# The scaling of the second norm's token rows on ScalarE: eight copies with a factor per partition

## The chip, the cores and the metric

The kernel runs on one core of one Trainium2 chip. The metric is the device time of one execution in microseconds. The kernel before took 679.23, 679.91 and 679.58 us in three runs, a median of 679.58.

## What is computed

One block of a vision tower over 4 images of 64 channels and 64 x 64 pixels, in float32. `h` starts as an involution (a 3 x 3 filter whose weights are computed from the pixel), with a class token ahead of it; a state-space layer on its norm is added; and last an expert layer on its second norm is added. The change lies in this last part:

```
h = h + ffn(layernorm(h))
ffn: H = gelu(x @ W1 + b1)                      64 -> 256 channels
     probs = softmax(H @ Wg + bg)               8 experts
     e = argmax(probs)
     out = probs[e] * (H @ Wd[e] + bd[e])       256 -> 64 channels
```

The layer norm has no weights: (x - mean) / sqrt(var + 1e-5) over the 64 channels of a token. The kernel takes the mean into W1 (a centering matrix is multiplied into it), so the rows only have to be multiplied by the factor 1 / sqrt(var + 1e-5).

## The kernel before

Stages with a barrier between them: set-up, involution, matrices of the state-space layer, its norm, the layer itself, and `experts` (line 1204). The change touches `experts` alone.

**Items.** The 16384 tokens are cut into 16 items of 1024 tokens, and a 17th has the four class tokens. `hT` holds the channels on partitions, with two tokens (a "par" each) side by side on 128 partitions, 512 columns an item. An item passes these steps; the letters in brackets name the engine.

- `turn_in` (L1316) [TensorE]: four transposes bring tokens onto partitions; `rest` (L1490) [ScalarE] copies the result out of PSUM into `hs`: 128 partitions x 8 groups x 64 channels.
- `minus_sum` (L1539) [VectorE] and `squares` (L1469) [ScalarE, eight activations with an accumulated sum] give sum and variance of every token; `factor` (L1675 to L1685) [GpSimd, six instructions on 128 x 8] gives the factor, `fac`.
- `normalise` (L1552) [VectorE]: one product of the 128 x 512 rows of `hs` with `fac`, broadcast along the channels, gives `xn`.
- `turn_out` (L1324) [TensorE]: four transposes back; `high` (L1461) [ScalarE] and `low` (L1545) [VectorE] split the result into a high part and a remainder, `u`.
- `hide(i, h)` for h = 0, 1 (L1335) [TensorE]: six matmuls with W1 into the two banks `pH`; `gelu(i, h)` (L1446) [ScalarE] reads each bank twice, four activations of 512 columns; `part` (L1531) [VectorE] makes the remainder.
- `judge` (L1351) [TensorE], `add_bg` (L1477) and `tanh` (L1483) [ScalarE], `gates` (L1361) [TensorE], `choose_best` and `weigh_best` (L1563 to L1595) [VectorE]: the gate.
- `speak(i, t)` for eight tiles t (L1382) [TensorE]: six matmuls give all eight experts' outputs of 128 tokens into one of three banks `pE`; `multiply(i, t)` (L1525) [VectorE] multiplies them by the gate, which is zero for all experts but one.
- `tree(i, k)` for k = 0, 1 (L1694, L1696, L1698, L1703) [GpSimd]: sums over the eight experts for four tiles, and adds `hs`; `keep_bias` (L1601) and `finish` (L1610) [VectorE] add the bias; a DMA stores the rows.

**The order.** Each engine's program is written out by hand as a loop over windows i = -3 to 16, and the engines meet only at semaphores; an engine carries out its own instructions in their order. In window i:

- TensorE: hide(i+1, 0), speak 0 and 1 of item i, hide(i+1, 1), speak 2, the transposed gate, turn_out(i+2), speak 3 and 4, judge(i+1), speak 5, gates(i+1), speak 6, the bias matmul, turn_in(i+4), speak 7. `hide(i, h)` waits until the gelus before it have emptied the banks (L1331); `speak` waits until the multiply three tiles earlier has emptied its bank (L1377); `judge` waits for all four `part` of the item (L1342).
- ScalarE: gelu(i+1, 0), gelu(i+1, 1), the copy of the gate, high(i+2), squares(i+3), add_bg(i+1), tanh(i+1), rest(i+4); in the very first window then two casts of the bias table (L1511, L1512).
- VectorE: multiply 0, keep_bias(i-1), part, multiply 1, part, minus_sum(i+3), multiply 2, two part, multiply 3, finish(i-1), multiply 4, low(i+2), multiply 5, choose_best(i+1), multiply 6, weigh_best(i+1), multiply 7, and last normalise(i+3). Behind the first window stands a subtraction on the bias table (L1662), which waits for the casts.
- GpSimd: tree(i, 0), factor(i+3), tree(i, 1). The first tree waits for multiply 3 (L1692), the factor for squares(i+3).

`normalise(i)` waits for `factored` of its item and for `turned_out` of the item before, since there is one `xn`; `turn_out(i)` waits for `normed`.

Of the kernel before, what the change touches and what calls it, by code (L numbers as in the profile page):

```python
# [6 lines left out]
ALU = mybir.AluOpType  # L7
ACT = mybir.ActivationFunctionType
# [7 lines left out]
F = HW  # L16
# [1187 lines left out]
def experts(nc, g):  # L1204
# [3 lines left out]
    NH = 6  # L1208
# [4 lines left out]
    with ExitStack() as ctx:  # L1213
        def sem(name):
            return ctx.enter_context(nc.semaphore("ex_" + name))

        def sb(name, shape, dt=F32):
            return ctx.enter_context(nc.sbuf_tensor("ex_" + name, shape, dt))
# [17 lines left out]
        hs = [sb(f"hs{n}", [128, TPI, F]) for n in range(NH)]  # L1236
# [3 lines left out]
        fac = [sb(f"fac{n}", [128, 4, TPI]) for n in range(2)]  # L1240
        xn = sb("xn", [128, TPI, F])
# [24 lines left out]
        newton, factored, normed = sem("newton"), sem("factored"), sem("normed")  # L1266
        turned_out, u_high, u_made = sem("turned_out"), sem("u_high"), sem("u_made")
# [14 lines left out]
        def there(i):  # L1282
            return 0 <= i < ITEMS

        def is_cls(i):
            return i == NCH

        def cols(i):
            return B if is_cls(i) else CH

        def rows(i):
            return B if is_cls(i) else 128

        def columns(i):
            return 1 if is_cls(i) else TILES

        def groups(i):
            return 2 * columns(i)

        def tiles(i):  # L1300
            return 1 if is_cls(i) else TPI
# [4 lines left out]
        with nc.Block() as block:  # L1306
# [129 lines left out]
            @block.scalar  # L1436
            def _(act):
                def gelu(i, h):
                    if i >= 2:
                        act.wait_ge(spoke, TPI * (i - 1))  # L1440
                    if i >= 1:
                        act.wait_ge(parted, 4 * (i - 1) + 2 * h + 2)
                    for par in range(2):
                        act.wait_ge(hidden, 4 * i + 2 * h + par + 1)
                        for o in (hidf, hid[i % 2][0]):
                            last = nc.scalar.activation(o[:, h, par, 0:cols(i)], pH[par][:, 0:cols(i)], ACT.Gelu,  # L1446
                                                        bias=g.b1c[:, h:h + 1])
                        last.then_inc(gelued, 1)

                def keep_gate(i):  # L1450
                    act.wait_ge(gate_turned, i + 1)
                    if i >= 1:
                        act.wait_ge(biased, i)
                    P = rows(i)
                    nc.scalar.copy(gT[:, 0:P], pT[:, 0:P]).then_inc(gate_kept, 1)

                def high(i):
                    act.wait_ge(turned_out, i + 1)
                    if i >= 2:
                        act.wait_ge(hidden, 4 * (i - 1))  # L1460
                    nc.scalar.copy(u[i % 2][0][:, 0:cols(i)], pXU[:, 0:cols(i)]).then_inc(u_high, 1)  # L1461

                def squares(i):
                    act.wait_ge(summed, i + 1)
                    if i >= 2:
                        act.wait_ge(factored, i - 1)
                    P = rows(i)
                    for t in range(groups(i)):
                        last = nc.scalar.activation(sq[0:P, i % 2, t, :], hs[i % NH][0:P, t, :], ACT.Square, scale=float(F),  # L1469
                                                    bias=stat[i % 2][0:P, 0, t:t + 1], accum_out=stat[i % 2][0:P, 1, t:t + 1])  # L1470
                    last.then_inc(squared, 1)

                def add_bg(i):
                    act.wait_ge(judged, i + 1)
                    if i >= 1:
                        act.wait_ge(gated, i)
                    nc.scalar.activation(level[:, 0:cols(i)], pGR[0:4 * EX, 0:cols(i)], ACT.Identity,  # L1477
                                         bias=g.bgc[:, 0:1]).then_inc(leveled, 1)

                def tanh(i):  # L1480
                    act.wait_ge(dv, GATE * i + 3)
                    P, T = rows(i), groups(i)
                    nc.scalar.activation(gl[0:P, 2, 0:T], gl[0:P, 0, 0:T], ACT.Tanh, scale=0.5).then_inc(tanhed, 1)  # L1483

                def rest(i):
                    act.wait_ge(turned_in, i + 1)
                    if i >= NH:
                        act.wait_ge(reduced, NB * (i - NH + 1))
                    P, n = rows(i), 128 * columns(i)
                    nc.scalar.copy(hs[i % NH][0:P, 0:groups(i), :].rearrange("p t f -> p (t f)"), pXU[0:P, 0:n]).then_inc(rested, 1)  # L1490

                act.wait_ge(w1_made, 1)
                nc.scalar.copy(W1P[0][:], pH[0][:, 0:HID]).then_inc(w1_made, 1)
                rest(0)
                for i in range(1 - AHEAD, ITEMS):
                    if there(i + 1):
                        gelu(i + 1, 0)
                        gelu(i + 1, 1)
                    if there(i):
                        keep_gate(i)  # L1500
                    if there(i + 2):
                        high(i + 2)
                    if there(i + 3):
                        squares(i + 3)
                    if there(i + 1):
                        add_bg(i + 1)
                        tanh(i + 1)
                    if there(i + 4):
                        rest(i + 4)
                    if i == 1 - AHEAD:  # L1510
                        nc.scalar.copy(bdh[lower], bd[lower])  # L1511
                        nc.scalar.copy(bdP[upper], bd[upper]).then_inc(bd_high, 1)  # L1512

            @block.vector
            def _(v):
# [26 lines left out]
                def low(i):  # L1542
                    v.wait_ge(u_high, i + 1)
                    c = slice(0, cols(i))
                    nc.vector.tensor_tensor(u[i % 2][1][:, c], pXU[:, c], u[i % 2][0][:, c], ALU.subtract).then_inc(u_made, 1)  # L1545

                def normalise(i):
                    P, T = rows(i), groups(i)
                    v.wait_ge(factored, i + 1)
                    if i >= 1:  # L1550
                        v.wait_ge(turned_out, i)
                    nc.vector.tensor_tensor(xn[0:P, 0:T, :], hs[i % NH][0:P, 0:T, :], fac[i % 2][0:P, 3, 0:T].unsqueeze(2).broadcast_to([P, T, F]),  # L1552
                                            ALU.mult).then_inc(normed, 1)

                def choose_best(i):
                    P, T = rows(i), groups(i)
# [56 lines left out]
                def window(i):  # L1613
                    now = tiles(i) if there(i) else 0
                    more = there(i + 1)
                    if now:
                        multiply(i, 0)
                    if there(i - 1):
                        keep_bias(i - 1)
                    if more:  # L1620
                        part(i + 1, 0, 0)
                    if now > 1:
                        multiply(i, 1)
                    if more:
                        part(i + 1, 0, 1)
                    if there(i + 3):
                        minus_sum(i + 3)
                    if now > 2:
                        multiply(i, 2)
                    if more:  # L1630
                        part(i + 1, 1, 0)
                        part(i + 1, 1, 1)
                    if now > 3:
                        multiply(i, 3)
                    if there(i - 1):
                        finish(i - 1)
                    if now > 4:
                        multiply(i, 4)
                    if there(i + 2):
                        low(i + 2)  # L1640
                    if now > 5:
                        multiply(i, 5)
                    if more:
                        choose_best(i + 1)
                    if now > 6:
                        multiply(i, 6)
                    if more:
                        weigh_best(i + 1)
                    if now > 7:
                        multiply(i, 7)  # L1650
                    if there(i + 3):
                        normalise(i + 3)

                nc.vector.memset(inverse[:, :, EX:], -float(EX)).then_inc(consts, 1)
                v.wait_ge(consts, 1)
# [109 lines left out]
```

## Time and profile before

| | us |
|---|---|
| median of three runs | 679.58 |
| lowest and highest | 679.23, 679.91 |
| the profiled execution, time | 679.56 |
| its span | 677.8 |
| TensorE busy | 593.3 (88%) |
| VectorE busy | 531.1 (78%) |
| GpSimd busy | 410.4 (61%) |
| ScalarE busy | 266.4 (39%) |

The span runs from the first to the last instruction that the profiler recorded; the device time is 1.8 us longer. The expert stage begins at 363 us of the span. Busy shares are means over all stages.

How to read the rows further down: PE is TensorE's matmuls, PEld its weight loads, DVE VectorE, ACT ScalarE, POOL GpSimd; L1552 is line 1552 of the kernel; after the arrow in brackets stands whose work ended the idle time before the instruction. On ScalarE, VectorE and TensorE an instruction's duration includes some tail that overlaps the next one's start, so the distance of two starts tells what an instruction costs in a row of its like.

### The profile page before, as it was taken

The numbers are of one execution on the slowest core, as the hardware profiler recorded it, in microseconds if no ns is written. First come the engines' busy times: TensorE is split into PE (matmuls) and PEld (weight loads), VectorE is DVE, ScalarE is ACT, GpSimd is POOL, SyncE is SP. The second block draws the span as 40 slices with busy tenths as digits, with TensorE's granted clock in tenths as the row PEclk, the third lists the DMA queues.
The fourth block names the chain that finished last, engine by engine and source line by source line (L and its number), as shares of the span: only waits on it lengthen the run. The fifth ranks groups of instructions, "written<-read, shape, count | busy, mean of one in ns | idle before, by whom it ended". The sixth has DMA issues, their size and how long they took to land. (4 is left out here: it accounts for less than half of the span.)

```text
span 677.8 us, 9715 instructions
## 1 busy us (share of the span) xinstructions
PE 593.3 (88%) x2998; PEld 436.9 (64%) x2998; DVE 531.1 (78%) x966; ACT 266.4 (39%) x691; POOL 410.4 (61%) x562
## 2 busy tenths in 40 slices
PE   0699999966995799999984599999999999999994
PEld 0477777754763688778763277766666666766672
DVE  6688888873596688888871378898889988888985
ACT  2132223223473122222223765555555555555310
POOL 1689999610154043333336248888878778888777
PEclk9999999995795999999997599999999999999998
DMA  6200000000000000000000000000000000000001
GB/s 252 49 2 0 0 1 1 0 0 1 0 0 1 0 1 0 1 0 0 1 0 0 1 1 16 16 17 15 17 15 12 6 15 16 17 16 16 15 17 31
DMA packets 13140, 9.78 MB, mean 14 GB/s; under 512 B 4524, under 2 KB 12844, under 8 KB 12844
## 3 DMA queue, kind: packets, MB, share of 16 engines
q1 hardware_dynamic: 13084, 9.29, 4.3%
q8 instruction: 19, 0.31, 0.2%
q14 instruction: 21, 0.17, 0.1%
q10 hardware_dynamic: 16, 0.00, 0.0%
HBM read 5.10 MB, written 4.20 MB: 14 GB/s over the span
## 5 line engine op out<-in xcount | busy, mean ns | idle before, releaser
L1382 PE MATMUL ex_pE<-ex_WdP,ex_hid 128*128 128x512 f32 x774 | 203.7, 405 | 0.0
L1382 PEld LDWEIGHTS ex_pE<-ex_WdP,ex_hid 128*128 128x128 f32 x774 | 138.8, 187 | 41.7 <-issue 10.9
L1694 POOL TENSOR_TENSOR ex_s<-ex_ms 128x1024 f32<-128x1024 f32 (+1 forms) x33 | 84.3, 2554 | 46.8 <-DVE ex_ms L1525 46.8
L1525 DVE TENSOR_TENSOR ex_ms<-ex_pE,ex_gate 128x512 f32<-128x512 f32 x129 | 87.8, 682 | 22.9 <-PE ex_pE L1382 22.5
L1195 POOL TENSOR_TENSOR hT<-hT,ssm_gelu 128x512 f32<-128x512 f32 x32 | 47.7, 1508 | 94.8 <-ACT ssm_gelu L1168 94.8
L723 DVE TENSOR_TENSOR inv_prod<-inv_pW,m_img 128x504 f32<-128x504 f32 x144 | 91.7, 681 | 17.1 <-PE inv_pW L638 15.4
L649 PE MATMUL inv_pS<-ident,inv_prod 128*128 128x128 f32 x576 | 87.5, 274 | 4.7 <-DVE inv_prod L723 4.7
L649 PEld LDWEIGHTS inv_pS<-ident,inv_prod 128*128 128x128 f32 x576 | 69.8, 140 | 27.2 <-DVE inv_prod L723 19.3
L638 PE MATMUL inv_pW<-inv_ysb,m_conv2L 98*128 98x512 f32 x144 | 69.4, 485 | 2.3 <-DVE inv_ysb L711 2.3
L1446 ACT ACTIVATE ex_hidf<-ex_pH,b1c 128x512 f32<-128x512 f32 (+1 forms) x68 | 45.1, 663 | 55.9 <-PE ex_pH L1335 55.9
L1151 ACT CAST ssm_z<-ssm_back 128x512 fp32r<-128x512 f32 x32 | 18.3, 618 | 101.5 <-DVE ssm_back L1127 101.5
L1065 PE MATMUL ssm_y<-ssm_z,N 128*128 128x512 f32 x192 | 51.9, 407 | 6.7 <-DVE ssm_z L1130 6.5
L1130 DVE TENSOR_TENSOR ssm_z<-ssm_back,ssm_z 128x512 fp32r<-128x512 f32 x32 | 36.1, 1170 | 19.3 <-ACT ssm_z L1151 19.3
L1531 DVE TENSOR_TENSOR ex_hid<-ex_hidf,ex_hid 128x512 fp32r<-128x512 f32 (+1 forms) x68 | 50.2, 758 | 1.2 <-ACT ex_hid L1446 1.2
L1032 PE MATMUL ssm_v<-u,LV 128*128 128x512 f32 (+1 forms) x192 | 50.5, 409 | 0.0
L1696 POOL TENSOR_TENSOR ex_s<-ex_s 128x512 f32<-128x512 f32 (+1 forms) x33 | 46.7, 1416 | 2.6
L1065 PEld LDWEIGHTS ssm_y<-ssm_z,N 128*128 128x128 f32 x192 | 36.5, 193 | 17.6 <-DVE ssm_z L1130 9.2
L1469 ACT ACTIVATE ex_sq<-ex_hs,ex_stat 128x64 f32<-128x64 f32 (+1 forms) x130 | 43.5, 345 | 7.1 <-DVE ex_stat L1539 7.1
L800 POOL TENSOR_TENSOR u<-ln_u,u 128x512 fp32r<-128x512 f32 x14 | 18.6, 1350 | 44.6 <-ACT u L869 44.6
L1446 ACT ACTIVATE ex_hid<-ex_pH,b1c 128x512 fp32r<-128x512 f32 (+1 forms) x68 | 45.2, 665 | 0.0
L1552 DVE TENSOR_TENSOR ex_xn<-ex_hs,ex_fac 128x512 f32<-128x512 f32 (+1 forms) x17 | 33.1, 1946 | 14.8 <-POOL ex_fac L1685 14.8
L1351 PE MATMUL ex_pGR<-ex_hid,ex_WgP 128*32 128x512 f32 (+1 forms) x136 | 34.4, 396 | 9.1 <-DVE ex_hid L1531 9.0
(242 smaller groups left out, 1048.3 us busy)
## 6 DMA issues: line engine op xcount, KB each, us to landing
m_img<-in_x SPq DMA_DIRECT2D x2, 2048.0 KB, 9.2
out<-ex_res SPq DMA_DIRECT2D x16, 256.0 KB, 2.2
WdT<-in_L_ffn_Wd SPq DMA_DIRECT2D x2, 256.0 KB
bd<-in_L_ffn_bd SPq DMA_DIRECT2D x16, 2.0 KB
W1d<-in_L_ffn_W SPq DMA_DIRECT2D x2, 64.0 KB
m_Bm<-in_L_attn_fwd_B_real SPq DMA_DIRECT2D x2, 16.0 KB, 2.0
m_Bm<-in_L_attn_fwd_B_imag SPq DMA_DIRECT2D x2, 16.0 KB, 2.0
m_Bm<-in_L_attn_bwd_B_real SPq DMA_DIRECT2D x2, 16.0 KB, 2.0
```

Source lines behind the costliest of these rows:

```text
L638: nc.tensor.matmul(pW[k % NW][:], m.conv2L[:, k, :], ysb[u][:], start=True, stop=True).then_inc(weighed, 1)
L649: last = nc.tensor.matmul(pS[:, 128 * j:128 * j + 128], prod[:, k, 2 * j:2 * j + 2, :], g.ident[:], is_transpose=True, start=(k == 0 and j ...
L723: nc.vector.tensor_tensor(prod[:, k, :, lo:hi], pW[k % NW][:, :, lo:hi], rows[:, :, lo + dw:hi + dw], ALU.mult).then_inc(filtered, 1)
L1032: last = nc.tensor.matmul(out[:], g.LV[weight][:, LVI[d][t][q], :], cols(g.u[value], b, d, h, q), start=(q == 0 and (value, weight) == PAR ...
L1065: last = nc.tensor.matmul(out, g.N[weight][:, n, d, first:first + 2, :], before(zP[n][value], d, h), start=False, stop=(n == 1 and (value, ...
L1195: nc.gpsimd.tensor_tensor(t, t, act_y[n % 4][:], ALU.add).then_inc(summed, 1)
L1382: last = nc.tensor.matmul(pE[n % 3][0:P].rearrange("p e f -> p (e f)"), hid[i % 2][value][:, h, par, 128 * j:128 * j + P], WdP[weight][:, ...
L1446: last = nc.scalar.activation(o[:, h, par, 0:cols(i)], pH[par][:, 0:cols(i)], ACT.Gelu, bias=g.b1c[:, h:h + 1])
L1525: nc.vector.tensor_tensor(ms[b % NB][0:P, t % TPB, :].rearrange("p (e f) -> p e f", e=EX), pE[n % 3][0:P], gate[i % 2][0:P, t, :].unsqueez ...
L1531: nc.vector.tensor_tensor(hid[i % 2][1][:, h, par, c], hidf[:, h, par, c], hid[i % 2][0][:, h, par, c], ALU.subtract).then_inc(parted, 1)
L1694: nc.gpsimd.tensor_tensor(s4[0:P, 0:T], m[:, :, 0:4 * F], m[:, :, 4 * F:], ALU.add).then_inc(halved, 1)
L1696: nc.gpsimd.tensor_tensor(s2[0:P, 0:T], s4[0:P, 0:T, 0:2 * F], s4[0:P, 0:T, 2 * F:], ALU.add).then_inc(quartered, 1)
```

## The change

The one VectorE product in `normalise` is replaced by up to eight ScalarE activations of the function Copy, one for each of the groups of 64 channels, each with its column of `fac` as a scale that is read per partition. The waits are the same. On VectorE the step stood at the end of window i, behind multiply 7; on ScalarE it stands at the end of window i too, behind `rest(i+4)`, and in the first window ahead of the two casts.

```diff
@@ scalar engine
+                def normalise(i):
+                    act.wait_ge(factored, i + 1)
+                    if i >= 1:
+                        act.wait_ge(turned_out, i)
+                    P = rows(i)
+                    for t in range(groups(i)):
+                        last = nc.scalar.activation(xn[0:P, t, :], hs[i % NH][0:P, t, :], ACT.Copy, scale=fac[i % 2][0:P, 3, t:t + 1])
+                    last.then_inc(normed, 1)
...
                     if there(i + 4):
                         rest(i + 4)
+                    if there(i + 3):
+                        normalise(i + 3)
                     if i == 1 - AHEAD:
                         nc.scalar.copy(bdh[lower], bd[lower])
@@ vector engine
-                def normalise(i):
-                    P, T = rows(i), groups(i)
-                    v.wait_ge(factored, i + 1)
-                    if i >= 1:
-                        v.wait_ge(turned_out, i)
-                    nc.vector.tensor_tensor(xn[0:P, 0:T, :], hs[i % NH][0:P, 0:T, :], fac[i % 2][0:P, 3, 0:T].unsqueeze(2).broadcast_to([P, T, F]),
-                                            ALU.mult).then_inc(normed, 1)
...
                     if now > 7:
                         multiply(i, 7)
-                    if there(i + 3):
-                        normalise(i + 3)
```

## Rows read from the trace of the kernel before

**Rows 1.** The page: busy us, share of the span and instructions.

```profile
PE 593.3 (88%) x2998; PEld 436.9 (64%) x2998; DVE 531.1 (78%) x966; ACT 266.4 (39%) x691; POOL 410.4 (61%) x562
```

**Rows 2.** The chain of waits: start us, us, engine, tile, line.

```profile
594.84 2.80 POOL ex_s L1694
...
612.73 2.80 POOL ex_s L1694
```

**Rows 3.** Timeline, same turn: start us, us, engine, line, operation [idle before].

```profile
594.84 2.79 POOL L1694 TENSOR_TENSOR ex_s<-ex_ms 128x1024 f32<-128x1024 f32 x1 [2.48 <-DVE ex_ms L1525]
...
603.55 0.20 POOL L1685 TENSOR_TENSOR ex_fac<-ex_fac 128x8 f32<-128x8 f32 x1
...
603.78 2.87 DVE L1552 TENSOR_TENSOR ex_xn<-ex_hs,ex_fac 128x512 f32<-128x512 f32 x1 [0.36 <-POOL ex_fac L1685]
...
606.58 0.68 DVE L1525 TENSOR_TENSOR ex_ms<-ex_pE,ex_gate 128x512 f32<-128x512 f32 x1
...
611.97 0.68 DVE L1525 TENSOR_TENSOR ex_ms<-ex_pE,ex_gate 128x512 f32<-128x512 f32 x1
```

**Rows 4.** Timeline of TensorE's weight loads: `hide(.., 1)` of windows 1, 2, 13, 14.

```profile
411.05 0.53 PEld L1335 LDWEIGHTS ex_pH<-ex_u,ex_W1P 64*128 64x128 f32 x6 [0.37 <-issue]
...
428.07 0.53 PEld L1335 LDWEIGHTS ex_pH<-ex_u,ex_W1P 64*128 64x128 f32 x6 [0.37 <-issue]
...
623.07 0.53 PEld L1335 LDWEIGHTS ex_pH<-ex_u,ex_W1P 64*128 64x128 f32 x6 [0.37 <-issue]
...
640.45 0.53 PEld L1335 LDWEIGHTS ex_pH<-ex_u,ex_W1P 64*128 64x128 f32 x6 [0.37 <-issue]
```

**Rows 5.** Timeline of ScalarE, two gelus of the class tokens, 4 columns.

```profile
657.23 0.26 ACT L1446 ACTIVATE ex_hid<-ex_pH,b1c 128x4 fp32r<-128x4 f32 x1
657.38 0.26 ACT L1446 ACTIVATE ex_hidf<-ex_pH,b1c 128x4 f32<-128x4 f32 x1
```

**Rows 6.** Timeline, first and fourth gelu of item 0, the weight load behind them.

```profile
377.38 0.69 ACT L1446 ACTIVATE ex_hidf<-ex_pH,b1c 128x512 f32<-128x512 f32 x1 [0.44 <-PE ex_pH L1335]
...
379.10 0.70 ACT L1446 ACTIVATE ex_hid<-ex_pH,b1c 128x512 fp32r<-128x512 f32 x1
...
379.91 0.95 PEld L1335 LDWEIGHTS ex_pH<-ex_u,ex_W1P 64*128 64x128 f32 x6 [3.29 <-issue]
```

**Rows 7.** Groups of ScalarE by form, scale and bias by pointer: busy, mean ns.

```profile
L673 ACT ACTIVATE inv_yf<-inv_pY,m_ysc 96x512 f32<-96x512 f32 x16 | 12.4, 775 | 17.7 <-PE inv_pY L629 17.7
```

**Rows 8.** Timeline of window 0: `hide(1, 1)`, first tree, last factor instruction.

```profile
394.03 0.54 PEld L1335 LDWEIGHTS ex_pH<-ex_u,ex_W1P 64*128 64x128 f32 x6 [0.37 <-issue]
...
399.37 2.40 POOL L1694 TENSOR_TENSOR ex_s<-ex_ms 128x1024 f32<-128x1024 f32 x1 [9.12 <-DVE ex_ms L1525]
...
407.70 0.20 POOL L1685 TENSOR_TENSOR ex_fac<-ex_fac 128x8 f32<-128x8 f32 x1
```

**Rows 9.** Timeline of the fill, windows -3 to 0: casts, normalise, squares, gelu.

```profile
369.22 0.62 ACT L1512 CAST ex_bdP<-bd 64x512 fp32r<-64x512 f32 x1
...
371.32 0.69 DVE L1552 TENSOR_TENSOR ex_xn<-ex_hs,ex_fac 128x512 f32<-128x512 f32 x1 [6.01 <-POOL ex_fac L1685]
372.04 0.69 DVE L1662 TENSOR_TENSOR ex_bdP<-bd,ex_bdh 64x512 fp32r<-64x512 f32 x1
...
373.70 0.35 ACT L1469 ACTIVATE ex_sq<-ex_hs,ex_stat 128x64 f32<-128x64 f32 x1
...
379.63 0.69 DVE L1552 TENSOR_TENSOR ex_xn<-ex_hs,ex_fac 128x512 f32<-128x512 f32 x1 [5.10 <-POOL ex_fac L1685]
...
391.20 0.69 ACT L1446 ACTIVATE ex_hidf<-ex_pH,b1c 128x512 f32<-128x512 f32 x1
```

**Rows 10.** Timeline of TensorE in the state-space stage, a long wait.

```profile
355.22 2.93 PE L1065 MATMUL ssm_y<-ssm_z,N 128*128 128x512 f32 x6 [2.86 <-DVE ssm_z L1130]
```

**Rows 11.** Busy time by stretch; after the brackets the granted clock's share.

```profile
355.00:356.50 1.50, 1.28 (x3) 1.10 (x4) 0.16 (x1) 0.00 (x0) 1.30 (x1) 0.50 0.00 0
```

**Rows 12.** Groups of ScalarE by form, a load of an activation table.

```profile
L357 ACT ACT_TABLE_LOAD x1 | 1.3, 1283 | 3.3 <-issue 3.3
```

## The prediction

> **What bounds the kernel now.** I read the page's busy table first. TensorE is busy for 88% of the span and ScalarE for 39% [rows 1]; that invites the thought that work moved to ScalarE is free. A share of the whole span cannot say that, so I read the chain of waits next. In the expert stage it repeats every 17.89 us: first half-tile tree of GpSimd, its factor computation, a stretch called "issue", VectorE's work, the same tree again [rows 2]. The kernel there is no queue of one engine but a loop through GpSimd and VectorE.
>
> The timeline of one turn gives its parts [rows 3]. I write T for the start of the first tree of a window. T is 594.84; the factors are ready at 603.75, 8.91 later; `normalise` starts on VectorE at 603.78 and holds it until the next multiply at 606.58, 2.80; from that multiply to the fourth one are 5.39; this one takes 0.68 and the next tree starts 0.08 after it. 8.91 + 0.03 + 2.80 + 5.39 + 0.76 = 17.89. So `normalise` is on the path, with all of its 2.80 us.
>
> The weight loads of the second half of `hide` tell how long the windows are [rows 4]. I call their start H. While TensorE itself is the limit, H comes every 17.02 us (411.05 to 428.07). From H = 411.05 (window 1) to H = 623.07 (window 13) are 212.02 us for twelve windows, 17.67 each: only 0.65 each, 7.8 in all, above what TensorE needs. That is all that a free normalise could give back there.
>
> **The removed part.** VectorE loses 2.80 us per window in the loop above, and everything behind it in its queue (multiply, bias, part) moves forward. The old loop shrinks to 15.1 and no longer binds.
>
> **The added part: eight copies.** The trace before has no ScalarE copy of 64 columns with a pointer to its factor. The nearest rows are the gelus, which have one pointer too (the bias). With 4 columns they follow each other at 0.15 us [rows 5], with 512 columns at (379.10 - 377.38) / 3 = 0.573 [rows 6], so a column costs 0.8 ns and 64 of them cost 0.15 + 0.05 = 0.20. Lower end: 0.15, if the 60 columns more are free. Upper end: an activation with two pointers lasts 775 ns [rows 7] against the 0.69 of a gelu, 0.09 more; if the copy has a second pointer too it is 0.29. I take 0.20, the form being the gelu's: 8 x 0.20 = 1.60 before the next instruction of ScalarE starts, with bounds 1.2 and 2.3; xn itself is complete at 7 x 0.20 + 0.31 = 1.71. The Trainium skill's page "ScalarE: Activation LUTs" (What ACT_TABLE_LOAD costs) gives 186 ns + 0.833 per column, 93 for a pointer and an overlap of 93; an estimate by it is 0.24 a copy, 1.92 for eight, and would put the sum below about 5 us higher. The same page (Rules for kernel authors) says to use VectorE for a plain multiplication; no row here shows the copy, and the sum below tests that rule in its place in the loop.
>
> **The added wait, and what stands behind it.** ScalarE's queue is in order. At the end of window i it now waits for the factors of item i+3, and behind that wait stand the four gelus of `gelu(i+2, 0)`. `hide(i+2, 1)` waits for these gelus, and behind it on TensorE stand all matmuls of the next `speak`. So a second loop comes into being:
>
> T to factors ready 8.91 [rows 3], hand-over 0.04, copies 1.60, four gelus 379.80 - 377.38 = 2.42, last gelu to weight load 379.91 - 379.80 = 0.11 [rows 6], H to the next T 399.37 - 394.03 = 5.34 [rows 8]. Sum 18.42.
>
> The last term is of window 0, where little but TensorE's order lies in it (hide, third speak, turn-out, fourth speak, then VectorE's fourth multiply). VectorE's other work of that stretch (bias, the first parts, the negative sum) fits before its third multiply, since VectorE comes 2.8 us earlier; GpSimd's second tree falls there too and may block a `part` for some tenths, which I leave to the range.
>
> 18.42 is above 17.02 and above 17.67. Twelve windows: H(13) - H(1) = 221.0 where it was 212.0, +9.0.
>
> **Window 0.** T to factors is 407.90 - 399.37 = 8.53 [rows 8], so H(1) = H(0) + 5.34 + 8.53 + 0.04 + 1.60 + 2.42 + 0.11 = H(0) + 18.04, where it was 17.02: +1.0.
>
> **The start.** Here the copies hurt most, because the pipeline is being filled and ScalarE's order is all there is. (a) `normalise(0)` runs at 371.32 [rows 9], for only 0.69 here, where GpSimd is quiet, and now until 372.93 on ScalarE, and the two casts of the bias table (0.62 each) come behind it: done at 374.17, not at 369.84. VectorE's subtraction that waits for them (0.69, begun at 372.04 before) ends at 374.9, the negative sum behind it at 375.6, and the squares of item 1 start at 375.65, not at 373.70: 1.95 late. (b) The factors of item 1 were ready just before `normalise(1)` at 379.63 [rows 9]; now at 381.58. ScalarE waits for them, copies until 383.2, and only then begins `gelu(0, 0)`, which had begun at 377.38 [rows 6], 2.2 before those factors existed: 5.8 late. From there `hide(0, 1)`, judge, gates and the rest of item 3 follow 5.8 late. (c) `normalise(2)` stands ahead of `gelu(1, 0)`: 391.20 [rows 9] + 5.8 + 1.6 = 398.6; gelus and hand-over 2.53, so H(0) = 401.13, where it was 394.03 [rows 8]: +7.1. Bounds: +5.5 if (a) is hidden, +9 with the upper price of a copy.
>
> **The end.** Item 16 has 4 rows and two copies of 0.2, so window 13 is TensorE's again: at most 17.02, where 640.45 - 623.07 = 17.38 [rows 4]: -0.4. Behind it nothing changes.
>
> No DMA is moved; the stores wait for `finish` and move with the windows. The pointer buffers (`fac`, `hs`, `xn`) have at least as long to live as before; `turned_out(i)` is given in the middle of the window and is no wait.
>
> **Sum.** +7.1 + 1.0 + 9.0 - 0.4 = +16.7, over 679.56, the profiled execution's time (span 677.8; the three runs' median is 679.58, the same): 696.3, and I say 696.5. The price of a copy counts eight-fold in 15 places: 1.2 instead of 1.60 gives 690, 2.3 gives 707. Contention of `part` with the second tree could add up to 0.3 in 12 windows, 4.
>
> **Rivals.**
>
> 1. *The relief wins.* ScalarE is idle for 61% [rows 1], the copies vanish in it, and the windows fall to 17.02: 679.6 - 7.8 - 0.4 = 671.4. This decides if the new loop stays within 17.02: 18.42 less the 1.60 of the copies is 16.82, so all eight copies would have to take 0.2 us together, or the factors to be ready 1.4 us earlier. The idle share of ScalarE speaks for it, the loop against it. 3 in 100.
>
> 2. *The loops balance.* The new loop equals the old windows of 17.67 if the eight copies take 0.85 together, 0.11 each; with a start that hides its waits the time would be some 680. The price of a gelu with 4 columns, 0.15 [rows 5], speaks against it. 3 in 100.
>
> 3. *Copies as dear as with two pointers*, or a longer one from SBUF: 2.3 per window, 705 to 708. 10 in 100.
>
> 4. *TensorE's clock falls.* The copies make it stand still for some 1.4 us more before H. The trace has one wait of 2.86 us, and behind it six matmuls took 2.93 us [rows 10] at a granted clock of 0.50, the lower level [rows 11]. If each window brought that, about 2 us more in 13 windows: 722. The new wait is half as long. 3 in 100.
>
> 5. *A table load for the copy*, 1.28 us as other functions had in the set-up [rows 12], once before the copies and once behind them in each window, 15 times: 39 more, 735. In the expert stage square, gelu, tanh and identity follow each other, and the trace has no load there. 1 in 100.
>
> **How the numbers follow.** The forecast has 80 in 100 and its time is 696.5. The range goes from the lower price of a copy, 690, to the upper one, 707, and leaves rivals 1, 2, 4 and 5 out. About 0.2% (1.4 us) can be told from no change. Faster 0.03, the same 0.03, slower 0.94.
>
> **What would show it.** In the profile after: (i) windows 1 to 13 about 18.4 us apart, H(1) near 419, H(13) near 640; (ii) the chain goes from the factors to ScalarE's copies and gelus, then TensorE's `hide` and `speak`, with no VectorE stretch of 2.8; (iii) `hide(.., 1)` waits for gelus, about 1.4 us; (iv) the wait of `judge` for `part` is gone; (v) the gelus of item 0 start near 383. Windows of 17.0 would make the loop wrong; windows of 18.4 with a start unchanged would make the steps (a) to (c) wrong; another pitch of copies only the price.

## The result and the profile after

The changed kernel takes 708.98 us in the median of four executions (703.59 to 713.02), the kernel before 679.75 in the four beside them. The ratio, which is not the quotient of the two medians, is 1.0405 (95% interval 1.0308 to 1.0503): slower. The direction was forecast; the size was not. The forecast was 696.5 with a range to 707; the profiled execution, at 703.59, lies inside it, the median 2 us above. Of the executions of the kernel before that stand beside the experiments, one took 1462.28 us; what held it up is not known, and ratios leave it out.

The page of the kernel after, its busy line (against [rows 1]). ScalarE gains only 3 points, and no engine is busier than 84%:

```profile
PE 592.8 (84%) x2998; PEld 438.8 (63%) x2998; DVE 510.6 (73%) x949; ACT 297.1 (42%) x821; POOL 406.1 (58%) x562
```

The chain of waits of the kernel after, one turn (start us, us, engine, tile, line; the lines behind 1498 are shifted by 1 on GpSimd and by 11 or less on VectorE, so L1695 is the first tree, L1678 the factor's power, L1536 the multiply):

```profile
511.75 1.78 ACT ex_xn L1498 x7
515.26 0.58 ACT ex_hid L1446
515.98 0.97 PE ex_pH L1335 x6
516.94 1.59 PE ex_pE L1382 x6
519.08 1.42 PE ex_pE L1382 x6
520.53 0.70 DVE ex_ms L1536
521.30 2.79 POOL ex_s L1695
...
527.45 1.66 POOL ex_fac L1678
530.51 1.78 ACT ex_xn L1498 x7
```

It is the loop of the forecast: first tree, factors, copies, gelus, `hide`, two `speak`, the fourth multiply, the tree. It repeats after 18.76 us where the old one took 17.89 [rows 2]. VectorE has one instruction in it.

The timeline of the same turn gives the terms (against [rows 3]):

```profile
511.26 0.20 POOL L1686 TENSOR_TENSOR ex_fac<-ex_fac 128x8 f32<-128x8 f32 x1
511.50 2.04 ACT L1498 ACTIVATE ex_xn<-ex_hs,ex_fac 128x64 f32<-128x64 f32 x8 [1.85 <-POOL ex_fac L1686]
...
513.44 0.67 ACT L1446 ACTIVATE ex_hidf<-ex_pH,b1c 128x512 f32<-128x512 f32 x1
...
515.15 0.68 ACT L1446 ACTIVATE ex_hid<-ex_pH,b1c 128x512 fp32r<-128x512 f32 x1
...
515.95 0.56 PEld L1335 LDWEIGHTS ex_pH<-ex_u,ex_W1P 64*128 64x128 f32 x6 [2.08 <-issue]
515.98 0.97 PE L1335 MATMUL ex_pH<-ex_u,ex_W1P 64*128 64x512 f32 x6 [1.67 <-ACT ex_hid L1446]
...
521.30 2.78 POOL L1695 TENSOR_TENSOR ex_s<-ex_ms 128x1024 f32<-128x1024 f32 x1 [3.21 <-DVE ex_ms L1536]
...
530.02 0.20 POOL L1686 TENSOR_TENSOR ex_fac<-ex_fac 128x8 f32<-128x8 f32 x1
```

Tree to factors 530.22 - 521.30 = 8.92; hand-over 0.04; copies 513.44 - 511.50 = 1.94; four gelus 515.83 - 513.44 = 2.39; to the weight load 0.12; from there to the tree 5.35. The sum is 18.76. All terms but the copies are within 0.03 of the forecast's; the copies take 1.94, not 1.60. TensorE waits 1.67 us for the last gelu, where about 1.4 was expected. The wait of `judge` for `part`, 23.3 us in all before, is down to 4.7.

Where the 24.0 us between the two profiled spans went, by the starts of `hide(.., 1)` (H) and the first instruction of the expert stage. From here on, window i of a profile is the stretch from H(i) to H(i+1):

| stretch | before | after | difference | forecast |
|---|---|---|---|---|
| start of the span to the expert stage | 362.86 | 364.41 | +1.5 | 0 |
| to H(0) | 31.17 | 39.32 | +8.2 | +7.1 |
| H(0) to H(1) | 17.02 | 18.35 | +1.3 | +1.0 |
| H(1) to H(13) | 212.02 | 225.14 | +13.1 | +9.0 |
| H(13) to H(14) | 17.38 | 16.60 | -0.8 | -0.4 |
| to the end | 37.35 | 37.98 | +0.6 | 0 |

H(1) stands at 422.08 and H(13) at 647.22, where 419 and 640 were forecast; the windows are 18.76 and not 18.4.

### The profile page after: what moved, and what is told of

Same layout as the page of the kernel before. It is cut to its first block and busy times, and to the rows that moved or that the text cites. A ratio compares the mean times of both kernels' runs of the same rounds, so it can differ in the third digit from the quotient of the medians.

```text
span 701.8 us, 9828 instructions
## 1 busy us (share of the span) xinstructions
PE 592.8 (84%) x2998; PEld 438.8 (63%) x2998; DVE 510.6 (73%) x949; ACT 297.1 (42%) x821; POOL 406.1 (58%) x562
## 5 line engine op out<-in xcount | busy, mean ns | idle before, releaser
L1536 DVE TENSOR_TENSOR ex_ms<-ex_pE,ex_gate 128x512 f32<-128x512 f32 x129 | 88.4, 687 | 55.2 <-PE ex_pE L1382 52.9
L1695 POOL TENSOR_TENSOR ex_s<-ex_ms 128x1024 f32<-128x1024 f32 (+1 forms) x33 | 82.8, 2509 | 67.7 <-DVE ex_ms L1536 67.7
L1542 DVE TENSOR_TENSOR ex_hid<-ex_hidf,ex_hid 128x512 fp32r<-128x512 f32 (+1 forms) x68 | 57.8, 870 | 18.2 <-ACT ex_hid L1446 18.1
L1335 PE MATMUL ex_pH<-ex_u,ex_W1P 64*128 64x512 f32 (+1 forms) x204 | 33.2, 429 | 30.3 <-ACT ex_hid L1446 30.3
L1498 ACT ACTIVATE ex_xn<-ex_hs,ex_fac 128x64 f32<-128x64 f32 (+1 forms) x130 | 33.2, 338 | 31.8 <-POOL ex_fac L1686 31.8
L1335 PEld LDWEIGHTS ex_pH<-ex_u,ex_W1P 64*128 64x128 f32 x204 | 17.9, 192 | 44.5 <-issue 43.4
L688 ACT COPY hT<-inv_pS 128x256 f32 (+1 forms) x32 | 10.5, 383 | 81.9 <-PE inv_pS L649 81.9
```

The lines of the kernel that those rows point to most:

```text
L1335: last = nc.tensor.matmul(pH[par][:, 0:cols(i)], W1P[weight][r, 128 * h:128 * h + 128], u[i % 2][value][r, 0:cols(i)], start=((value, weig ...
L1498: last = nc.scalar.activation(xn[0:P, t, :], hs[i % NH][0:P, t, :], ACT.Copy, scale=fac[i % 2][0:P, 3, t:t + 1])
L1536: nc.vector.tensor_tensor(ms[b % NB][0:P, t % TPB, :].rearrange("p (e f) -> p e f", e=EX), pE[n % 3][0:P], gate[i % 2][0:P, t, :].unsqueez ...
L1542: nc.vector.tensor_tensor(hid[i % 2][1][:, h, par, c], hidf[:, h, par, c], hid[i % 2][0][:, h, par, c], ALU.subtract).then_inc(parted, 1)
L1695: nc.gpsimd.tensor_tensor(s4[0:P, 0:T], m[:, :, 0:4 * F], m[:, :, 4 * F:], ALU.add).then_inc(halved, 1)
```

## The experiments

Two things were open: whether the loss is the loop through the copies, and what makes executions of one kernel differ by 10 us. The times of the kernel before beside the first four runs are 675.90 to 684.72, median 680.73 (680.39 without the execution of 1462.28), and beside the others nearly the same; so 0.2% is finer than these runs tell.

**The changed kernel again.** No edit.

> The changed kernel unchanged, for its spread: four executions took 703.59 to 713.02, with a mean granted clock of 0.941 in the fastest and 0.920 in the slowest. Theory clock: the spread is TensorE's clock, which falls in some windows of some executions while TensorE waits before hide(.., 1); then the executions lie between 703.5 and about 714, their times rise with a falling mean clock (about 9 us for 0.02), and a profile of a slower one has stretches at 0.50 in the expert stage. Rival chance: the spread is of the machine and comes in other stages too; then the profile's extra time does not stand in the expert stage and the times do not follow the clock.

Six executions: 703.06 to 711.83, median 710.59, ratio 1.0430 (1.0376 to 1.0485); mean granted clocks 0.936 in the fastest, 0.922 in the slowest. The profile is of an execution of 707.81. Its windows 1 to 12 are 18.71 to 18.73 us but for two, 461.08 to 481.38 and 481.38 to 501.68, of 20.30. TensorE's timeline in the first of them, and the granted clock there (the third number from the right):

```profile
461.12 0.96 PE L1335 MATMUL ex_pH<-ex_u,ex_W1P 64*128 64x512 f32 x6 [1.65 <-ACT ex_hid L1446]
462.00 2.53 PE L1382 MATMUL ex_pE<-ex_WdP,ex_hid 128*128 128x512 f32 x6
...
464.54 1.06 PE L1324 MATMUL ex_pXU<-ident,ex_xn 128*128 128x128 f32 x4
```

```profile
461.00:462.00 1.00, 0.89 (x6) 0.53 (x6) 1.00 (x3) 0.00 (x0) 1.00 (x1) 1.00 0.00 0
...
464.00:465.00 1.00, 1.00 (x6) 0.80 (x5) 0.43 (x1) 0.81 (x3) 0.00 (x0) 0.50 0.00 0
...
466.00:467.00 1.00, 1.00 (x6) 0.81 (x5) 0.46 (x1) 1.00 (x6) 0.00 (x0) 1.00 0.00 0
```

Behind a wait of 1.65 us the six matmuls of `hide` still ran at 2.4 GHz; then the granted clock fell to 0.50, the level of 1.2 GHz, and the next six matmuls took 2.53 us. In the first profile of this kernel a wait of 1.77 us in the same window had no such effect:

```profile
459.71 0.96 PE L1335 MATMUL ex_pH<-ex_u,ex_W1P 64*128 64x512 f32 x6 [1.77 <-ACT ex_hid L1446]
460.61 1.67 PE L1382 MATMUL ex_pE<-ex_WdP,ex_hid 128*128 128x512 f32 x6
```

So the clock falls in some windows of some executions, at 1.57 us a time. It does not make up the whole difference: of the 4.2 us by which this execution is longer than the first profile, 3.1 are the two windows and 1.4 the start, where the clock rose later and H(0) stands 40.77 us behind the stage's start, not 39.32.

**The copies moved behind the first gelus.**

```diff
-                        gelu(i + 1, 1)
+                    if there(i + 2):
+                        normalise(i + 2)
+                    if there(i + 1):
+                        gelu(i + 1, 1)
...
-                    if there(i + 3):
-                        normalise(i + 3)
```

> The eight copies of item i+2 stand between gelu(i+1, 0) and gelu(i+1, 1) of window i, where ScalarE waits for hide(i+1, 1) anyway, not at the end of window i-1. Theory loop: the time of the changed kernel comes from the copies and the wait for the factors ahead of gelu(.., 0); moved behind it they leave the loop, windows fall to TensorE's 17.0 us, the start is about 1.5 us behind the kernel before: 671 to 675, faster than both, spread small. Rival price: a ScalarE activation of 64 columns is dear wherever it stands; then windows stay above 18 us and the time above 690.

Twelve executions: 669.07 to 678.03, median 675.85 beside 680.73, ratio 0.9916 (0.9883 to 0.9948). Windows 0 to 11 are 17.01 to 17.02 us long. The timeline shows why: the copies begin when the fourth gelu of the first half has been given out, and `hide(.., 1)` starts during them:

```profile
518.34 0.70 ACT L1446 ACTIVATE ex_hid<-ex_pH,b1c 128x512 fp32r<-128x512 f32 x1
518.91 2.02 ACT L1498 ACTIVATE ex_xn<-ex_hs,ex_fac 128x64 f32<-128x64 f32 x8
519.42 0.53 PEld L1335 LDWEIGHTS ex_pH<-ex_u,ex_W1P 64*128 64x128 f32 x6 [0.37 <-issue]
520.82 0.68 ACT L1446 ACTIVATE ex_hidf<-ex_pH,b1c 128x512 f32<-128x512 f32 x1
```

The same eight copies, as dear as before, cost nothing here: the place in ScalarE's queue is what costs. The median missed the expected 671 to 675 by 0.9 us, and the spread, 9.0 us, is not small. In the profiled execution the start was 3.9 us longer than before (H(0) 35.11 behind the stage's start, against 31.17), not 1.5. The gelus of item 0 begin 1.5 us late, as expected; the copies of item 1 ahead of `gelu(0, 1)` add 0.4; and about 2 come from the clock, which rose later in this execution: `turn_in`, `hide(1, 0)` (1.65 us, not 0.97) and the first two `speak` ran wholly or partly at 1.2 GHz.

**Every copy twice.**

```diff
+                        nc.scalar.activation(spare[0:P, t, :], hs[i % NH][0:P, t, :], ACT.Copy, scale=fac[i % 2][0:P, 3, t:t + 1])
                         last = nc.scalar.activation(xn[0:P, t, :], hs[i % NH][0:P, t, :], ACT.Copy, scale=fac[i % 2][0:P, 3, t:t + 1])
```

> Every copy is made twice, the second time into a tile that nobody reads; all else as in the changed kernel. Theory loop: each window grows by the whole 1.95 us, from 18.75 to 20.7, and the start by twice that: about +29 us, 733, in an execution whose clock stays up. Theory clock: the wait of TensorE before hide(.., 1) grows from 1.7 to 3.6 us, so the clock falls in many or all windows: 745 or more, and the granted clock of the expert stage well below 1. Rival slack: ScalarE has room and the loop is elsewhere; then under 715.

Median 757.29 (750.08 to 758.33), ratio 1.1141 (1.1083 to 1.1198), mean clock 0.90 to 0.91. One window of the profile, window 8 (582.58 to 603.20), is 20.62 us long, 1.87 above 18.75: nearly the whole 1.94 of the eight copies. The nine others of windows 3 to 12 are 22.08 to 22.23, 1.5 more, and there the clock fell to its lower level behind the longer wait (windows 1 and 2, at 23.23 and 23.53, are longer still):

```profile
516.12 1.65 PE L1336 MATMUL ex_pH<-ex_u,ex_W1P 64*128 64x512 f32 x6 [3.55 <-ACT ex_hid L1447]
517.70 1.65 PE L1383 MATMUL ex_pE<-ex_WdP,ex_hid 128*128 128x512 f32 x3
```

**The first three items on VectorE.** Items 0 to 2 keep the old product in its old place.

```diff
-                    if there(i + 3):
+                    if i >= 0 and there(i + 3):
                         normalise(i + 3)
...
+                    if i < 0:
+                        normalise(i + 3)
```

> Items 0 to 2 are normalised by VectorE as before the change, items 3 to 16 by ScalarE's copies. Theory loop with the fill priced by itself: the start is that of the kernel before, windows 1 to 13 stay at 18.75 us; 703.6 minus 7 to 8.5: 695 to 697 with the clock up. Rival: the fill's delay is hidden behind something later, then 702 to 704.

Median 700.14 (696.03 to 704.28), ratio 1.0291 (1.0225 to 1.0358). H(0) stands 31.16 us behind the start of the stage, as in the kernel before to 0.01, and windows 1 to 10 are 18.7 to 18.8. The fastest execution is 7.0 us below the fastest of the changed kernel. So 7 to 8 us of the change's cost are the start, by its three normalisations alone. Windows 11 and 12 of this profile are 20.28 and 20.32 and window 13 is 18.19 in place of 16.6: falls of the clock.

**TensorE kept busy in its wait.**

```diff
+                    if now == TPI and more:
+                        n = TPI * i + 2
+                        if n >= 3:
+                            pe.wait_ge(chosen, n - 2)
+                        for _ in range(10):
+                            nc.tensor.matmul(pE[n % 3][:].rearrange("p e f -> p (e f)")[:, 0:HID], W1P[0][:, 0:128], W1P[0][:],
+                                             start=True, stop=True)
                     if more:
                         hide(i + 1, 1)
```

> Ahead of hide(i+1, 1) TensorE makes ten matmuls of 256 columns more into the PSUM bank that speak 2 overwrites next, about 1.1 us that lie inside its wait of 1.67 us for the gelus; results unchanged. Theory clock: the executions of the changed kernel above 703 are those in which the clock falls in this wait, 1.57 us a time (windows of 20.30 instead of 18.73 in the profile of the run again); kept busy it does not fall, so the time is about 703 with a spread of 1 or 2 us above it, median 703 to 706 where the changed kernel had 710, mean clock at 0.93 or above. Rival chance: the spread and the median stay at 703 to 712. Rival issue: the added matmuls push hide(.., 1) back, then the windows of the profile are longer than 18.8.

Median 707.44 (701.37 to 709.45), ratio 1.0348 (1.0305 to 1.0390), mean clocks 0.930 to 0.946. Windows 1 to 12 are 18.73 to 18.75. In the stretches H(13) to H(14) and H(14) to H(15) (i = 14 and 15 of the edit), where no wait had been, the added matmuls cost 1.2 us each (17.78 and 17.19 for 16.59 and 16.00). The median is 1.4 above the expected 703 to 706; less these 2.4 it lies inside. The run was made again without them, with the changed kernel as its partner:

> The changed kernel once more, as the partner of the next run on the same chip. Theory clock: executions between 703 and 713, median about 710, mean clock 0.92 to 0.93 in the slower ones; a profile above 704 has windows of 20.3 us among those of 18.7.

> The ten added matmuls of 256 columns stand only in windows 0 to 13, where TensorE waits for the gelus, and no more in windows 14 and 15, where nothing waits and they cost 1.2 us each. Theory clock: as in the first run of this kind but 2.4 us less: median 704 to 706, fastest 699 to 701, 4 to 6 us below its partner; all windows of the profile 18.7. Rival chance: no difference to the partner beyond 1 us.

The changed kernel: median 707.16 (705.52 to 712.20), ratio 1.0375 (1.0321 to 1.0428), windows 2 and 3 of 20.33 and 20.32 and window 13 of 18.12 in place of 16.60. Kept busy: median 704.43 (699.55 to 706.42), ratio 1.0308 (1.0256 to 1.0361), no window of 1 to 13 above 18.75. The difference of the medians is 2.7 us, less than the 4 to 6 expected, and that of the means is 4.7 (708.35 and 703.63); the intervals of the ratios overlap. Ahead of H(0) the added matmuls met no wait in this profile and cost something there too: H(0) stands 41.95 us behind the stage's start, 40.22 in its partner. That the clock falls behind the wait is shown by the profiles. That filling the wait prevents it fits them (two of the three of the changed kernel have windows of 20.3, neither of the two with the filled wait has one), but so few profiles do not prove it, and what the falls cost in the median, some 3 to 5 us, is uncertain by as much.

Another part of the spread comes ahead of what the change touches: the expert stage began at 358.9 to 367.7 us in these profiles, and the kernel before has a spread of 9 us too. The slowest profile of the changed kernel, at 712.20, is 8.6 us above the first: 4.7 by its three falls, 3.3 by the later start of the stage, 0.9 by the time to H(0).

**The scale as a constant, and as a bias.**

```diff
-                        last = nc.scalar.activation(xn[0:P, t, :], hs[i % NH][0:P, t, :], ACT.Copy, scale=fac[i % 2][0:P, 3, t:t + 1])
+                        last = nc.scalar.activation(xn[0:P, t, :], hs[i % NH][0:P, t, :], ACT.Copy, scale=0.5)
```

> The eight copies multiply by a constant, 0.5, and not by the factor of the row; the wait for the factors stays. The computation is changed: the rows are not scaled by their factors. Theory pointer: a copy costs 0.24 us because of its pointer, 0.15 to 0.16 without it; then the windows are 0.6 to 0.7 us shorter, 18.1, and the fastest execution about 694. Rival source: the 0.24 is that of any small activation from SBUF; windows stay at 18.7 and the fastest at 703. Theory loop, in either case: windows shorten by eight times what one copy saves.

```diff
-                        last = nc.scalar.activation(xn[0:P, t, :], hs[i % NH][0:P, t, :], ACT.Copy, scale=fac[i % 2][0:P, 3, t:t + 1])
+                        last = nc.scalar.activation(xn[0:P, t, :], hs[i % NH][0:P, t, :], ACT.Identity, bias=fac[i % 2][0:P, 3, t:t + 1])
```

> The eight activations are Identity with the factor as bias, by pointer, and a constant scale of 1. The computation is changed: the factor is added to the row and not multiplied. If a pointer costs the same in either place the distance of two is 0.24 us, windows 18.7; if the bias pointer is the cheaper one, as the gelus with 4 columns led to think, it is 0.20 and windows are 18.4.

**The source in PSUM.**

```diff
-                        last = nc.scalar.activation(xn[0:P, t, :], hs[i % NH][0:P, t, :], ACT.Copy, scale=fac[i % 2][0:P, 3, t:t + 1])
+                        last = nc.scalar.activation(xn[0:P, t, :], pXU[0:P, F * t:F * t + F], ACT.Copy, scale=fac[i % 2][0:P, 3, t:t + 1])
```

> The eight copies keep their scale by pointer but read 64 columns of the PSUM bank pXU and not hs. The computation is changed: the rows of another item are scaled. If the source explains why the gelu's 0.15 (with one pointer, 4 columns, from PSUM) led to 0.20 while the copy from SBUF takes 0.243, the starts are now 0.20 apart and windows 18.4. If they stay at 0.24, the gelu is the exception for another reason, such as a pointer that does not change.

The eight activations in the timelines of the three, in this order:

```profile
502.26 1.28 ACT L1498 ACTIVATE ex_xn<-ex_hs 128x64 f32<-128x64 f32 x8 [1.85 <-POOL ex_fac L1686]
```

```profile
508.60 2.02 ACT L1498 ACTIVATE ex_xn<-ex_hs,ex_fac 128x64 f32<-128x64 f32 x8 [1.85 <-POOL ex_fac L1686]
```

```profile
513.72 1.74 ACT L1498 ACTIVATE ex_xn<-ex_pXU,ex_fac 128x64 f32<-128x64 f32 x8 [1.86 <-POOL ex_fac L1686]
```

One activation lasts 241, 333 and 326 ns (medians), so the distance of two starts is (1.28 - 0.24) / 7 = 0.148, (2.02 - 0.33) / 7 = 0.241 and (1.74 - 0.33) / 7 = 0.202 us; in the changed kernel (2.04 - 0.34) / 7 = 0.243. A pointer costs 0.09, in either place; the source in SBUF costs 0.04 more than in PSUM. The windows follow: 17.99, 18.72 and 18.47 us, and 8 x 0.095 = 0.76 is the 18.75 - 17.99. The run with the constant has a median of 689.70 (686.23 to 691.69), ratio 1.0115 (1.0066 to 1.0164), its fastest execution 686.23 where 694 was expected. The profiled one, 688.21, is 15.4 below the 703.59 of the changed kernel: 3.5 by the earlier start of the stage (360.86 against 364.41), 1.9 in the time to H(0) (37.42 against 39.32), 0.7 in window 0 (17.61 against 18.35) and 9.2 in windows 1 to 12 (215.97 against 225.14). The other two, each executed once, took 701.95 and 703.53.

The Trainium skill's page "ScalarE: Activation LUTs" (What ACT_TABLE_LOAD costs) gives 93 ns for a pointer and 186 + 0.833 ns per column for the rest, 239 and 333 ns for these forms; the traces agree, with 241 and 333 to 336.

**The late copies with the first three items on VectorE.** The two edits together.

```diff
+                    if i > 0 and there(i + 2):
+                        normalise(i + 2)
                     if there(i + 1):
                         gelu(i + 1, 1)
...
+                    if i < 0:
+                        normalise(i + 3)
```

> Items 0 to 2 normalised by VectorE as before the change, items 3 to 16 by ScalarE between gelu(i+1, 0) and gelu(i+1, 1). Theory loop: windows at 17.0 us from window 1 on as in the run late, and the start of the kernel before: 1 to 3 us below the run late, median 672 to 675, fastest 668. Rival: the start is no shorter, since the three copies' place there is hidden, and the time is that of late, 676.

Seven executions: 667.26 to 672.25, median 670.87 beside 680.86, ratio 0.9847 (0.9816 to 0.9878): faster than either kernel, 1.5% below the kernel before, and its interval lies below 1. H(0) is 31.16 us behind the start of the stage and windows 0 to 11 are 17.0. The median is 1.1 us below the expected 672 to 675. From H(0) to H(14) the profile has 237.5 us, the kernel before 246.4: the 8.9 us between are the gain of the loop. The timeline, with GpSimd's last factor instruction and the copies, shows that the factors are ready 1.5 us before the copies begin (507.60 to 509.10), and that `hide` does not wait for the copies:

```profile
507.40 0.20 POOL L1697 TENSOR_TENSOR ex_fac<-ex_fac 128x8 f32<-128x8 f32 x1
...
508.52 0.70 ACT L1446 ACTIVATE ex_hid<-ex_pH,b1c 128x512 fp32r<-128x512 f32 x1
509.10 2.02 ACT L1498 ACTIVATE ex_xn<-ex_hs,ex_fac 128x64 f32<-128x64 f32 x8
509.61 0.53 PEld L1335 LDWEIGHTS ex_pH<-ex_u,ex_W1P 64*128 64x128 f32 x6 [0.37 <-issue]
```

## Why the forecast was right and wrong

- **The old loop, 17.89 with 2.80 for the product.** Right. With the product gone from VectorE and the copies out of the way the windows are TensorE's 17.02.
- **A second loop through the copies.** Right: the chain of waits after shows it, the copies made twice lengthen a window by their price, the copies moved leave it.
- **The price of a copy, "I take 0.20, the form being the gelu's: 8 x 0.20 = 1.60".** This is the step that failed: the term was mis-sized. It measured 0.243 and 1.94. The gelu reads PSUM, the copy SBUF, and that is the 0.04. The kernel before had a nearer row that I did not put into the sum: `squares`, also 128 x 64 from SBUF with one pointer, 0.23 to 0.24 from its start to the next instruction's (366.69 to 366.92 below). The forecast speaks of 15 places where the eight copies count; its own sum has 16, three in the start, one in window 0 and twelve after it. Sixteen times 0.34 is 5.4 us (1.0 + 0.3 + 4.1 by the table), which makes 701.7 of the 696.3. With the 1.5 us ahead of the expert stage and the 0.2 by which the last two rows of the table differ from the forecast, this is 703.4, against the 703.59 of the profiled execution. The estimate by the Trainium skill's page, 0.24, was the better one. ScalarE's timeline in the kernel before, one `squares`:

```profile
366.69 0.33 ACT L1469 ACTIVATE ex_sq<-ex_hs,ex_stat 128x64 f32<-128x64 f32 x1
366.92 0.19 ACT L1469 ACTIVATION_READ_ACCUMULATOR ex_sq<-ex_hs,ex_stat 128x1 f32 x1
```

- **The start.** Right in its mechanism, the three copies' waits: +8.2 against +7.1, and 3 x 0.34 is the difference. That it fits so closely is in part luck of the execution: in two other profiles of the changed kernel H(0) stands 0.9 and 1.4 us later, by the clock. Undone by itself the start gives 7 us back.
- **Window 13 and the end.** -0.8 and +0.6 against -0.4 and 0; the 1.5 before the expert stage lies in work that the change does not touch.
- **Rival 4, the clock, with "the new wait is half as long" and 3 in 100.** This step failed too. The clock fell, not in each window as the rival had it but in none to three of a profile, at 1.57 us and not 2. The sum held for an execution without such a fall, and even with the right price of the copy, 701.7, it is 7 us short of the median of 708.98. How much of the 5.4 us between the profiled execution and the median are falls stays open, since the slower executions beside it have no profile; the other profiles have falls, a later start of the stage and a later H(0), and the run with the filled wait puts the falls at some 3 to 5 us. Without so much the median would lie at 704 to 706, inside the range.
- **Rivals 1 and 2, relief.** Wrong as stated; but the run with the copies moved shows that the relief is there, 0.65 a window, once ScalarE's order lets it through.
- **Rivals 3 and 5.** A copy has one pointer, not the price of two; but the other half of rival 3, a longer one from SBUF, came true with 0.04 of the 0.09 that it allowed. No table load stands in the expert stage after.

The Trainium skill's page "ScalarE: Activation LUTs" (Rules for kernel authors) says to leave multiplications to VectorE. By the operation alone, 0.69 against 1.94, that holds. In the loops of this kernel the product took VectorE 2.80, and the copies in the right place took nothing: the measurement decides for ScalarE there.

## What to carry to other kernels

Before work is moved to an idle engine, write down what stands behind it in that engine's queue: a wait at the end of an iteration holds up the first work of the next one, and here the same eight instructions cost 1.7 us a window or nothing by their place alone. Take the price of an operation from a row that agrees with it in size, pointers and the memory of its source, all three. Where a change adds a wait to TensorE, read more than one profile: the first one here had no fall of the clock and two later ones had two and three. And compare medians with medians; the kernel before spreads over 9 us as well.

## What the runs showed of the hardware

- An activation of 64 columns starts 0.148 us after its like with constants and 0.243 with a pointer, both from SBUF; 0.202 with a pointer and a source in PSUM.
- TensorE's granted clock fell to the lower level behind waits of 1.65 us in some windows, where six matmuls took 2.53 us in place of 1.67, and did not behind 1.77 us in another of the same kernel; with waits of about 3.55 us it was low behind nine of ten.
- The stages that the change does not touch differ by up to 9 us between executions (expert stage from 358.86 or from 367.74 us). The kernel before, with one profile, spreads by as much in its whole time.
